# Output projection of three batches moved from behind the attention loop into its steps

## The reference

```python
xn = layernorm(x)
q, k, v = heads of xn @ q_w, xn @ k_w, xn @ v_w
scores = (q * sigmoid(unity)) @ k.T / sqrt(16)
scores = where((j % 4 == 0) | (abs(i - j) <= 8), scores, -inf)
out = (softmax(scores) @ v) merged over heads        # [B, S, 256]
attn = out @ o_w + o_b                               # the output projection
ffn = fp8(xn) @ w8.T + bias
result = x + attn + ffn
```

## Time and profile before

| what | value |
|---|---|
| median of 3 runs | 1150.86 us (1149.98 to 1151.96) |
| profiled execution | 1153.22 us, span 1151.4 us |
| TensorE busy | 1080.5 us (94%) |
| VectorE busy | 944.7 us (82%) |
| ScalarE busy | 808.6 us (70%) |
| GpSimd busy | 249.3 us (22%) |

### The profile page before, as it was taken

The page is one execution under the profiler, slowest core; times in us unless marked ns, Lnnn a source line. Parts: engine busy times, 40 slices in busy tenths (PEclk is TensorE's granted clock), DMA queues, the critical chain, the costliest instruction groups (busy, mean ns, idle before and its releaser), DMA issues.

```text
span 1151.4 us, 28768 instructions
## 1 busy us (share of the span) xinstructions
PE 1080.5 (94%) x10944; PEld 492.7 (43%) x10944; DVE 944.7 (82%) x1203; ACT 808.6 (70%) x1524; POOL 249.3 (22%) x381
## 2 busy tenths in 40 slices
PE   5899999947999999999999999999999999999896
PEld 3566666512333333333333334333333333333585
DVE  5888777475999999999999999999999999998132
ACT  2443444215888888888888888888888888888500
POOL 1433333210221222122121212212121212212100
PEclk9999999956999999999999999999999999999998
DMA  6677777662223333333333333333333333232367
GB/s 190 190 230 229 218 229 235 197 194 66 90 85 110 96 102 91 109 96 94 101 105 98 91 96 113 94 95 97 109 95 92 100 104 101 89 104 85 97 247 271
DMA packets 192506, 150.74 MB, mean 131 GB/s; under 512 B 35628, under 2 KB 171564, under 8 KB 192364
## 3 DMA queue, kind: packets, MB, share of 16 engines
q1 hardware_dynamic: 188424, 142.10, 40.4%
q10 hardware_dynamic: 3952, 6.88, 1.7%
HBM read 79.86 MB, written 67.77 MB: 128 GB/s over the span
## 4 chain that ended last, share of the span: by engine, by line
PE 66%; DVE 10%; SPq 8%; issue 7%; DMA 6%; ACT 1%; POOL 0%; ACTq 0%; DVEq 0%; POOLq 0%
PE ps_attend L1127 16%; PE ps_attend L1057 12%; PE ps_attend L1092 9%; DVE peak_far L1002 9%; PE ps_attend L1134 6%; SPq L262 5%; PE ps_attend L1067 4%; PE ps_attend L1103 3%; DMA heads<-attn_dram 3%; PE ps_attend L1070 3%; SPq L256 3%; PE ps_project L582 2%; PE ps_project L551 2%; PE ps_project L572 2%; PE ps_attend L1110 2%
## 5 line engine op out<-in xcount | busy, mean ns | idle before, releaser
L1002 DVE TENSOR_REDUCE peak_far<-ps_attend 128x2 f32<-128x1024 f32 x512 | 608.6, 1221 | 55.1 <-PE ps_attend L1092 51.5
L934 ACT ACTIVATE probs<-ps_attend 128x512 f32<-128x512 f32 x1024 | 539.1, 597 | 54.9 <-PE ps_attend L1057 51.8
L1127 PE MATMUL ps_attend<-probs,v_op 128*32 128x512 f32 x2048 | 273.4, 606 | 0.0
L1057 PE MATMUL ps_attend<-q_op,k_op 51*128 51x512 f16 x1024 | 259.5, 387 | 14.4 <-DMA q_op<-negmax_rows 10.7
L1092 PE MATMUL ps_attend<-k_op,q_op 48*128 48x512 f16 x1024 | 186.6, 389 | 17.1 <-DVE peak_far L1002 15.5
L1057 PEld LDWEIGHTS ps_attend<-q_op,k_op 51*128 51x128 f16 x1024 | 77.8, 93 | 209.3 <-ACT probs L934 135.6
L939 ACT ACTIVATE probs<-ps_attend 108x512 f32<-108x512 f32 x256 | 138.9, 594 | 37.3 <-PE ps_attend L1070 37.3
L798 POOL CAST negmax<-peak 128x16 bf16<-128x16 f32 x64 | 12.6, 197 | 638.0 <-DVE peak L985 638.0
L1005 DVE TENSOR_REDUCE peak_near<-ps_attend 128x8 f32<-128x864 f32 x128 | 131.0, 1023 | 11.3 <-PE ps_attend L1110 11.1
L789 POOL TENSOR_TENSOR out_rows<-out_rows,share_rows 128x512 f32<-128x512 f32 x64 | 81.3, 1270 | 48.6 <-DMA share_rows<-shares_dram 46.0
L1067 PEld LDWEIGHTS ps_attend<-mask_q,mask_k 48*108 48x108 bf16 x1024 | 59.9, 125 | 67.8 <-ACT probs L934 55.3
(11 more groups left out here) (80 smaller groups left out, 1043.2 us busy)
## 6 DMA issues: line engine op xcount, KB each, us to landing
v_dram<-v_sb SPq DMA_DIRECT2D x64, 256.0 KB, 4.1
share_rows<-shares_dram SPq DMA_DIRECT2D x64, 256.0 KB
attn_dram<-out_rows SPq DMA_DIRECT2D x64, 256.0 KB, 5.7
v_op<-v_dram SPq DMA_DIRECT2D x48, 288.0 KB
q_dram<-qk_parts SPq DMA_DIRECT2D x96, 128.0 KB
k_dram<-qk_parts SPq DMA_DIRECT2D x96, 128.0 KB
q_op<-q_dram SPq DMA_DIRECT2D x128, 96.0 KB, 2.4
k_op<-k_dram SPq DMA_DIRECT2D x64, 144.0 KB, 3.1
```

What stands on the lines that cost most here:

```text
L934: ins = nc.scalar.activation(probs[:, r, h], ps_s[st.bank(kind)], ACT.Exp, scale=undo)
L1002: ins = nc.vector.tensor_reduce(peak_far[:, :, p, tile], banks, AX_X, ALU.max)
L1057: nc.tensor.matmul(bank, k[half(f, KM), keys], q[half(f, KM), p], start=True, stop=True).then_inc(s_ready, 1)
L1127: ins = nc.tensor.matmul(ps_o[h * VW:(h + 1) * VW], v[:, r, h * VW:(h + 1) * VW], probs[:, r, h], start=(r == 0), stop=False)
```

## The change

The 12 chunks of the first three batches are projected inside the steps of the batches behind them, in halves of 256 positions. There are 24 halves, in steps 17, 19, ... 63; `out_part` gives the half of a step. A half is a new entry `("out",)` of the list of score banks, behind `("negmax",)`: four matmuls (eight records) into one of the three score banks, a copy by ScalarE into `y_rows`, and an addition of `y_rows` to `base` by GpSimd. SP loads `heads` in steps 16, 20, ... 60 (`fetch_heads`) behind the move of the negative maxima, and stores each finished chunk (512 KB) in steps 20, 24, ... 64 at the end of its step; both are on SP's queue. Behind the steps only the last batch's four chunks are projected; their heads are loaded by SP in steps 64, 65, 66 and after them. ScalarE issues no loads any more.

```diff
-    ("near", 0), ("far", 2, 0), ("negmax",), ("far", 3, 1), ("far", 3, 0),
+    ("near", 0), ("far", 2, 0), ("negmax",), ("out",), ("far", 3, 1), ("far", 3, 0),
...
+OUT_FIRST, OUT_EVERY = G * CPB + 1, 2
...
+def out_part(s):
+    if not (OUT_FIRST <= s < STEPS and (s - OUT_FIRST) % OUT_EVERY == 0):
+        return None
+    return (s - OUT_FIRST) // OUT_EVERY
...
 def gpsimd_attend(pool):
...
+            if out_part(st.n) is not None:
+                part = out_part(st.n)
+                rows = base[:, part // 2, part % 2 * CH:(part % 2 + 1) * CH]
+                pool.wait_ge(bias_added, part // 2 + 1)
+                pool.wait_ge(s_used, st.entry(("out",)))
+                nc.gpsimd.tensor_tensor(rows, rows, y_rows[:, part % 2], ALU.add).then_inc(part_added, 1)
...
 def sync_attend(sp):
...
+        def fetch_heads(b, n):
+            for k in range(OUTS):
+                sp.wait_ge(attn_stored[k], 16 * len(range(k, ((b + 1) * G - 1) * CPB + n + 1, OUTS)))
+            for i in range(KC):
+                load_heads(sp, b, n, i)
...
-            elif st.at(3) < STEPS + CPB:
-                if st.at(3) == STEPS:
-                    for k in range(OUTS):
-                        sp.wait_ge(attn_stored[k], 16 * len(range(k, G * CPB, OUTS)))
-                for i in range(KC):
-                    load_heads(sp, 0, st.slot(3), i)
...
             if ("negmax",) in st.entries():
                 move_negmax(st)
+            if st.n >= G * CPB and (st.n % CPB == 0 or st.n >= STEPS):
+                b, n = (st.n // (G * CPB) - 1, st.n // CPB % CPB) if st.n < STEPS else (B - 1, st.n - STEPS)
+                fetch_heads(b, n)
+            if out_part(st.n - 1) is not None and out_part(st.n - 1) % 2 == 1:
+                part = out_part(st.n - 1)
+                sp.wait_ge(part_added, part + 1)
+                sp.dma_start(out_tiles[part // 2], totals[:, part // 2]).then_inc(out_stored, 16)
...
 def scalar_attend(act):
...
+                elif kind[0] == "out":
+                    part = out_part(st.n)
+                    if part >= 2:
+                        act.wait_ge(part_added, part - 1)
+                    ins = nc.scalar.activation(y_rows[:, part % 2], ps_s[st.bank(kind)], ACT.Copy)
...
 def tensor_attend(pe):
...
+        def score_out(st):
+            kind = ("out",)
+            part = out_part(st.n)
+            n = part // 2 % CPB
+            bank = free_score(st, kind)
+            pe.wait_ge(heads_loaded[n], 16 * KC * (part // 2 // CPB + 1))
+            for t in range(2):
+                tile = 2 * (part % 2) + t
+                for i in range(KC):
+                    ins = nc.tensor.matmul(bank[:, t * H:(t + 1) * H], heads[:, n, i, tile * P:(tile + 1) * P],
+                                           keep["wo"][:, i], start=(i == 0), stop=(i == KC - 1))
+            ins.then_inc(s_ready, 1)
...
             def maxima():
                 if ("negmax",) in st.entries():
                     score_peaks(st)
+                if ("out",) in st.entries():
+                    score_out(st)
...
-        for n in range(CPB):
-            project(0, n)
-        with pe.Fori(1, B - 1) as j:
-            for n in range(CPB):
-                project(j, n)
         for n in range(CPB - 1):
-            project(B - 1, n)
+            project(n)
```

More of the change, by code:

```diff
@@ L628 @@
 )
-SCORES = tuple(kind + (2 * pair[-1] + f,) if pair != ("negmax",) else pair
-               for pair in SCORE_PAIRS for kind in (pair[:-1],) for f in range(2 if pair != ("negmax",) else 1))
-ENTRIES = len(SCORES)
+SCORES = tuple(kind + (2 * pair[-1] + f,) if kind else pair
+               for pair in SCORE_PAIRS for kind in (pair[:-1],) for f in range(2 if kind else 1))
+OUT_FIRST, OUT_EVERY = G * CPB + 1, 2
 OPENS = {next(k for k in SCORES if k[:-1] == kind) for kind in {k[:-1] for k in SCORES if len(k) > 1}}
@@ L639, in entries @@
 def entries(s):
-    return [kind for kind in SCORES
-            if (-1 <= s and s + 1 < STEPS if kind == ("negmax",) else 0 <= s < STEPS)]
+    there = {("negmax",): -1 <= s and s + 1 < STEPS, ("out",): out_part(s) is not None}
+    return [kind for kind in SCORES if there.get(kind, 0 <= s < STEPS)]
+def out_part(s):
+    if not (OUT_FIRST <= s < STEPS and (s - OUT_FIRST) % OUT_EVERY == 0):
+        return None
+    return (s - OUT_FIRST) // OUT_EVERY
 def part_attend(nc, io, dram, keep, out, ctx, done):
@@ L684, in begun @@
                 return sum(len(entries(s)) for s in range(FIRST, self.at(d)))
-            return ENTRIES * self.at(d) + 1
+            return len(SCORES) * self.at(d) + 1
         def entry(self, kind, d=0):
@@ L744, in part_attend @@
     heads_loaded = [sem(f"heads_loaded{i}") for i in range(CPB)]
+    part_added = sem("part_added")
     y_ready = sem("y_ready")
@@ L748, in part_attend @@
     out_stored = sem("out_stored")
-    heads = keep["heads"]
+    heads = sb("heads", [P, CPB, KC, CH])
+    y_rows = sb("y_rows", [P, 2, CH])
     ps_y = [ps[:, 2 * i:2 * i + 2] for i in range(CPB)]
@@ L847, in move_negmax @@
                              negmax_rows[f * n:(f + 1) * n, st.n % 2]).then_inc(negmax_loaded, 16)
+        totals = keep["base"].rearrange("p (c t) f -> p c t f", t=TT)
+        def fetch_heads(b, n):
[3 more added lines that the diff above has]
+                load_heads(sp, b, n, i)
         def load_piece(st, piece):
@@ L898, in body @@
                 move_negmax(st)
+            if st.n >= G * CPB and (st.n % CPB == 0 or st.n >= STEPS):
[5 more added lines that the diff above has]
+                sp.dma_start(out_tiles[part // 2], totals[:, part // 2]).then_inc(out_stored, 16)
         unrolled(body)
[L901 to L904, removed]
+        fetch_heads(B - 1, CPB - 1)
+        for n in range(CPB - 1):
+            sp.wait_ge(total_ready, n + 1)
+            sp.dma_start(out_tiles[(B - 1) * CPB + n], totals[:, (B - 1) * CPB + n]).then_inc(out_stored, 16)
         for t in range(TT):
-            sp.wait_ge(total_ready, B * CPB + t)
+            sp.wait_ge(total_ready, CPB + t)
             sp.dma_start(out_tiles[B * CPB - 1, :, t], totals[:, B * CPB - 1, t]).then_inc(out_stored, 16)
@@ L953, in scalar_attend @@
         unrolled(body)
-        for k in range(OUTS):
-            act.wait_ge(attn_stored[k], 16 * len(range(k, (B - 1) * G * CPB, OUTS)))
-        with act.Fori(1, B - 1) as j:
-            for n in range(CPB):
-                act.wait_ge(y_ready, CPB * j + n - CPB + 1)
-                for i in range(KC):
-                    load_heads(act, j, n, i)
-        for n in range(CPB):
[L962 to L967, removed]
     def vector_attend(dve):
@@ L1013, in vector_attend @@
         dve.wait_ge(bias_added, B * CPB)
[L1015 to L1023, removed]
         for n in range(CPB - 1):
-            total(B - 1, n)
+            rows = base[:, (B - 1) * CPB + n]
+            dve.wait_ge(y_ready, n + 1)
+            nc.vector.tensor_tensor(rows, ps_y[n].rearrange("p a f -> p (a f)"), rows, ALU.add).then_inc(total_ready, 1)
         for t in range(TT):
             rows = keep["base"][:, B * S // P - TT + t]
-            dve.wait_ge(y_ready, B * CPB + t)
+            dve.wait_ge(y_ready, CPB + t)
             nc.vector.tensor_tensor(rows, last_y[t][:, 0:H], rows, ALU.add).then_inc(total_ready, 1)
@@ L1193, in body, with project @@
             far_unit(0, 1)
[L1195 to L1202, removed]
+        def project(n):
+            pe.wait_ge(heads_loaded[n], 16 * KC * B)
+            if n == 0:
+                pe.wait_ge(s_used, Step(0, STEPS).begun())
                 pe.wait_ge(u_used, 2 * UNITS * STEPS)
@@ L1217, in tensor_attend @@
         unrolled(body)
-        for n in range(CPB):
-            project(0, n)
-        with pe.Fori(1, B - 1) as j:
-            for n in range(CPB):
-                project(j, n)
         for n in range(CPB - 1):
-            project(B - 1, n)
+            project(n)
         pe.wait_ge(heads_loaded[CPB - 1], 16 * KC * B)
         for t in range(TT):
-            pe.wait_ge(total_ready, (B - 1) * CPB + (t >= 2))
+            if t >= 2:
+                pe.wait_ge(total_ready, 1)
             for i in range(KC):
@@ L1259, in build @@
             "undo": sb("undo", [P, 1]),
-            "heads": sb("heads", [P, CPB, KC, CH]),
             "peak_far": sb("peak_far", [P, 2, PAIRS, TT]),
```

## The result

The changed kernel takes 1172.49 us (median of 4 runs, 1171.42 to 1173.1) against 1151.07 for the kernel before (its median with a fourth run): ratio 1.0185, 95% interval 1.017 to 1.02. It is slower by 1.85%, 5 us above the predicted time and inside the range. The profiled execution took 1172.05 us with a span of 1170.2, 18.8 us more than the span before.

A forecast was written before the change was run, and what follows sets the result against it. TensorE was taken to set the pace in the steps and the end: 1153.2 profiled + 47.5 for halves - 30.8 at the end = 1169.9, or 1167.5 us from the median of the runs; range 1152 to 1182.

The forecast's parts named there:

- A microsecond on TensorE behind line 1048 lies on the chain.: In the steps: VectorE's later wait doesn't absorb it; 1.98 us a half, 47.5 us for 24.
- The copy ahead of the exp costs the 0.25 above the columns.: In a step with a half: ScalarE's copy out delays the exp, 0.25 us above 1.73 of columns.
- The transfers cost nothing, since the half covers them.: SP's queue in the steps: the inserted half delays the reciprocal, so loads and stores cost nothing.
- My bound of 24 for the failing cover: Steps after a 1 MB burst: reciprocal late by up to 2 us in each of 12, 0 to 24 us.
- rival B: In the steps: 1 MB bursts make the reciprocal or negmax load late, 1176 to 1192 us; chance 13%.
- The end is 37.6 us.: Last copy out to span's end: last batch's chain, 37.6 us instead of 68.4, between 32.9 and 44.4.
- the prediction's middle: In the end: the middle, 26.9 us of 24.2 to 31.4, until the last chunk's heads have landed.
- The 1.7 us for a chunk at half clock: Last chunk in the end: half of the up to 3.5 us more it takes at the 1.2 GHz level.
- Rival A: In the steps: VectorE's pace absorbs the halves, say 0.9 us each, 1142 us; chance 13%.
- Rival E: In the steps: GpSimd's additions hold up VectorE's reciprocal, 24 x 1.27 = 30 us more, 1198 us; chance 2%.
- The port rule of the Trainium skill: GpSimd and VectorE share ports: two-SBUF-input or two-port-mode VectorE instructions block, reductions never; up to 1.27 us a step.

The follow-up runs named there:

- The early place: Half moved from behind line 1048 to early in the step, behind row 0's far scores, against the kernel with the store two steps later: 1220.61 us.
- one matmul: Each half keeps only its first of four matmuls, against the changed kernel; copy, addition and transfers stay: 1162.3 us, one run.
- transfers alone: Halves left out altogether (matmuls, copy, addition), loads of heads and stores kept in the steps, against the changed kernel: 1156.56 us, one run.
- halves with transfers ahead: Against the kernel with nine chunks moved in halves: loads and stores issued ahead of the sums, store two steps behind its half: 1181.36 us.

## Why the prediction held

- *A microsecond on TensorE behind line 1048 lies on the chain.* Right: a whole half, one with a quarter of its columns, and a quarter of a chunk cost 1.95, 0.66 (13.34) and 0.92 us there. The 24 halves cost 46.8 us against 47.5 forecast, 1.95 each against 1.98.
- *The copy ahead of the exp costs the 0.25 above the columns.* The chain shows it: behind the half come 0.47 us of ScalarE's wait and copy, then the exp, then the matmul. The sizes agree: what a half costs above its columns is 0.22 us here, 0.23 with a quarter of its columns (0.66 - 0.43), and 0.05 for a quarter of a chunk, whose copy is shorter.
- *The transfers cost nothing, since the half covers them.* The cover is there and is worth far more than I gave it: 3.7 us of late sums with it, 34 without. My bound of 24 for the failing cover was too low, because a wait of TensorE also cost clock (3.3 us of waiting, then 4.8 us at 0.50). This term was mis-sized: 0 forecast, 3.7 measured. It was rival B in a mild form.
- *The end is 37.6 us.* It is 35.3, a gain of 33.1 against 30.8. The total was nearly right, its steps weren't, and that is partly luck. The sums, sent behind 512 KB of share_rows and rows for attn_dram, took 5.0 us instead of 2.6; the store of shares, behind two loads of heads and a last store of 512 KB, took 4.7 instead of 2.0 (2.3 in the run with that store two steps later). So share_rows went out at 11.2 instead of 6.1 to 8.3. Then the last store of rows landed in 2.8 us instead of 5.7, and the last chunk's heads were sent at 20.8 us, where the prediction's middle has 20.6 (26.9 - 5.7 - 0.65; its own terms add up to 26.5 rather than 26.9): two misses that cancel. I followed the last chunk's own chain; the second chunk's load stands behind the last share_rows in SP's queue, and from its landing on TensorE runs three chunks in a row, 12.3 us, at the lower clock at first. TensorE was idle for half of the end, not most of it. The 1.7 us for a chunk at half clock fit the 2.0 and 1.8 lost behind the two gaps; nowhere was it the whole 3.5.
- *Rival A* needed less than 1.28 us a half. The early place showed how little VectorE's wait hides: 1.61 us a half, 0.12 below its columns. *Rival E*: GpSimd's addition (1047.62) runs beside a VectorE reduction and ahead of the multiplication, inside which the reciprocal at 1049.34 takes 0.34 us. The 44 reciprocals from 480 to 1080 us take 0.332 to 0.347 us, 0.332 to 0.334 in the kernel before, and the reductions 1.221 us in both. The port rule of the Trainium skill (SBUF — State Buffer, "Who interferes with whom") took nothing here that the trace shows.
- *The 5 us between 1167.5 and 1172.49.* From profile to profile I forecast 16.7 us and it is 18.8: 3.0 more in the steps, 1.4 ahead of the first half, 2.3 less at the end. The other 2.6 are the profiles' distance from the medians, 2.2 above before and 0.4 below after; the forecast carried the first over to the second. What is left is the later median of the kernel before, 0.2 us above the first.

## What to carry to other kernels

Moving work from a stretch that one engine sets into another that the same engine sets buys nothing by itself: price both ends, and what the moved work covered where it was. Move only as much as leaves the bare end just covered; here nine chunks instead of twelve, in quarters early in the step, with the stores apart from the loads, turned 1.85% slower into 0.3% faster. With a piece of work move its loads, and don't send bulk loads shortly ahead of a small transfer that an engine waits for.

## What the runs showed of the hardware

A wait of TensorE of 3.3 us was followed by 4.8 us at a granted clock of 0.50, and the step lost 5.6 us. Of the 32 steps behind bursts or loads in three runs (one matmul, transfers alone, halves with transfers ahead), the 22 in which the granted clock fell last 15.2 to 18.2 us and the ten in which it didn't 13.5 to 15.1. An 8 KB store whose completion took 2.0 us took 6.9 behind 1 MB on the same queue, with two loads of q and two of k issued right behind it.
